# Splitting and moving the one-time ternary rounding of the feed-forward weights in an attention and feed-forward kernel

## What is computed

```python
def absmean_quant(w):
    scale = jnp.mean(jnp.abs(w))
    mask = (jnp.abs(w) >= scale * 0.7).astype(w.dtype)
    return jnp.sign(w) * mask
w1_q = absmean_quant(w1)          # (2048, 512)
w2_q = absmean_quant(w2)          # (512, 2048)
h = gelu(x @ w1_q.T + b1); out = h @ w2_q.T + b2
lambda_full = exp(sum(lq1 * lk1)) - exp(sum(lq2 * lk2)) + LAMBDA_INIT
attn = rmsnorm(attn) * subln_weight * (1.0 - LAMBDA_INIT)   # then @ Wo.T
```

## Time and profile before

| | |
|---|---|
| device time, median of 3 runs | 4300.87 us (4296.52 to 4306.44) |
| device time of the profiled execution | 4298.3 us |
| its span | 4296.5 us |
| busy in it: PE, DVE, ACT, POOL | 3484.7, 3382.8, 2880.2, 1437.2 us |
| mean granted clock of TensorE | 0.926 of full speed |
| block 0 begins at | 87.6 us |

### The profile page before, as it was taken

The page is one execution under the profiler, slowest core; times in us unless marked ns, Lnnn a source line. Parts: engine busy times, 40 slices in busy tenths (PEclk is TensorE's granted clock), DMA queues, the critical chain, the costliest instruction groups (busy, mean ns, idle before and its releaser), DMA issues.

```text
span 4296.5 us, 81536 instructions
## 1 busy us (share of the span) xinstructions
PE 3484.7 (81%) x23454; PEld 2095.0 (49%) x23454; DVE 3382.8 (79%) x6194; ACT 2880.2 (67%) x6784; POOL 1437.2 (33%) x1564
## 2 busy tenths in 40 slices
PE   2688888888888887888788888888878878888886
PEld 1355544455445454545544544445544555444553
DVE  6788977888678886888767887778877889778881
ACT  1577766777567775677756777667766777567772
POOL 1243233332332324433343323432234432333323
PEclk6899999999999999999999999999999999999998
DMA  3100011000011001100011000101011000111000
GB/s 130 41 18 30 19 33 33 31 17 29 25 33 33 18 30 33 33 20 28 21 33 33 26 27 18 39 25 33 20 34 33 25 23 20 34 33 33 15 29 12
DMA packets 146817, 128.38 MB, mean 30 GB/s; under 512 B 66608, under 2 KB 117680, under 8 KB 145840
## 3 DMA queue, kind: packets, MB, share of 16 engines
q1 hardware_dynamic: 146352, 122.79, 8.8%
HBM read 67.61 MB, written 55.12 MB: 29 GB/s over the span
## 4 chain that ended last, share of the span: by engine, by line
PE 41%; DVE 20%; issue 20%; ACT 12%; POOL 5%; DMA 1%; SPq 1%; DVEq 1%; ACTq 1%; POOLq 0%
PE M L837 9%; DVE NM L682 6%; PE M L887 6%; PE SP_ L852 6%; PE F L924 6%; PE F L909 5%; PE DP L864 4%; DVE NM L690 3%; ACT E L554 3%; ACT DT L566 2%; ACT L571 2%; PE M L831 2%; DVE CC L702 1%; PE DX L864 1%; PE SP_ L853 1%
## 5 line engine op out<-in xcount | busy, mean ns | idle before, releaser
L554 ACT ACTIVATE E<-SP_,NM 128x256 f32<-128x256 f32 (+7 forms) x2048 | 1520.4, 743 | 1020.3 <-DVE NM L690 533.8
L852 PE MATMUL SP_<-KST,QST 96*128 96x512 f16 (+3 forms) x3072 | 838.2, 344 | 459.2 <-ACT E L554 385.4
L682 DVE TENSOR_REDUCE NM<-SP_ 128x1 f32<-128x896 f32 (+3 forms) x1024 | 1031.9, 1017 | 225.0 <-PE SP_ L853 218.5
L705 DVE SCALAR_TENSOR_TENSOR E<-E,CC 128x512 f32<-128x512 f32 (+7 forms) x1024 | 942.2, 920 | 36.2
L864 PE MATMUL DP<-ident,E 128*128 128x128 f32 x3328 | 585.1, 292 | 112.8 <-DVE E L705 97.2
L852 PEld LDWEIGHTS SP_<-KST,QST 96*128 96x128 f16 x3072 | 277.9, 101 | 793.8 <-ACT E L554 531.1
L690 DVE TENSOR_REDUCE NM<-SP_ 128x2 f32<-128x1024 f32 (+3 forms) x512 | 419.4, 819 | 244.8 <-PE SP_ L853 239.5
L566 ACT ACTIVATE DT<-DP 128x512 f32<-128x512 f32 (+3 forms) x1024 | 524.8, 513 | 127.8 <-PE DP L864 121.4
L837 PE MATMUL M<-WQKV,WT 128*128 128x512 f32 x1040 | 538.4, 611 | 10.3 <-DVE TOK L746 5.3
L909 PE MATMUL F<-X2H,W1Q 128*128 128x256 f16 x2048 | 501.4, 283 | 39.4 <-ACT HP L613 21.7
L864 PEld LDWEIGHTS DP<-ident,E 128*128 128x128 f32 x3328 | 389.8, 149 | 277.8 <-issue 125.8
(11 more groups left out here) (94 smaller groups left out, 4726.9 us busy)
## 6 DMA issues: line engine op xcount, KB each, us to landing
scratch<-SPL SPq DMA_DIRECT2D x65, 576.0 KB, 2.8
QST<-scratch SPq DMA_DIRECT2D x390, 64.0 KB, 2.4
X<-in_x SPq DMA_DIRECT2D x66, 256.0 KB, 2.7
out<-SQ SPq DMA_DIRECT2D x64, 256.0 KB, 2.0
KST<-scratch SPq DMA_DIRECT2D x390, 32.0 KB, 1.9
DT<-in_w2T SPq DMA_DIRECT2D x1, 4096.0 KB, 25.7
KST<-in_w1T SPq DMA_DIRECT2D x2, 1024.0 KB, 12.0
WQKV<-in_wqT SPq DMA_DIRECT2D x1, 1024.0 KB, 7.1
```

The costliest lines, as they stand in the source:

```text
L554: act.activation(dst, score_out(i, 2 * n + k, w), ACT.Exp, bias=NM[:, (2 * u + k) % 8:(2 * u + k) % 8 + 1], scale=1.0, accum_out=SUM[:, i ...
L682: nc.vector.tensor_reduce(NM[:, m:m + 1], score_out(i, 2 * n + k, P * (i + 1)), AX.X, ALU.max, negate=True).then_inc(max_ready, 1)
L705: nc.vector.scalar_tensor_tensor(out=E1[:, u % 4, 0:w], in0=E2[:, u % 2, 0:w], scalar=CC[:, u % 4:u % 4 + 1], in1=E1[:, u % 4, 0:w], op0=A ...
L852: pe.matmul(SP_[:, k[a // 512], 0:n], q, KST[0:ROWS, a // P:(a + n) // P, kk, :], start=True, stop=not last)
```

## The change

The raw weights go to buffers that are needed later: w1 to DT (tiles 0 to 3), to the upper half of KST (tiles 4 to 7) and to X1, w2 to DT (tiles 4 to 7), HH and HL. The sums of magnitudes are taken by ScalarE (Abs with accumulation). In the setup only chunks 0 and 1 of w1 are cut, by DVE as before. The other two chunks of w1 and all four of w2 are cut inside blocks 0 and 1: the first compare on GpSimd (low_cut), the second on DVE (late_cut). The scaling of Wo, w2's magnitudes and threshold move into block 0. DVE does layernorm before it scales Wq and waits for each load apart; the loads are issued in another order; the clearing of QST moves behind the first rstd on POOL.

```diff
+ABS_AT = (14, 16, 18, 20)
+LOW_AT = ((0, 2), (0, 8), (1, 2), (1, 8), (1, 15), (1, 21))
+CUT_AT = ((0, 6), (0, 12), (1, 6), (1, 12), (1, 20), (1, 26))
+WO_AT, ABS_TOTAL, ABS_PRODUCT, THR_AT = 15, 24, 26, 28
...
+        self.raw = kind == "first"
...
+        kraw = KST[:, TILES // 2:TILES, :, :].rearrange("p a b c -> p (a b c)").bitcast(F32)
+        draw = DT[:, :, :, :].rearrange("p a b c -> p (a b c)")
+        w1f = [draw[:, 0:FF], draw[:, FF:2 * FF], kraw, X1[:, :, :].rearrange("p a b -> p (a b)")]
+        w2f = [draw[:, 2 * FF:3 * FF], draw[:, 3 * FF:4 * FF], HH[:, :, :].rearrange("p a b -> p (a b)").bitcast(F32),
                HL[:, :, :].rearrange("p a b -> p (a b)").bitcast(F32)]
-        cutt = HP[:, :, :].rearrange("p a b -> p (a b)")
+        raw = (w1f, w2f)
+        cut = [q[:, :, :].rearrange("p a b -> p (a b)") for q in (W1Q, W2Q)]
+        low = HP[:, :, :].rearrange("p a b -> p (a b)").bitcast(BF16).rearrange("p (a b) -> p a b", a=2)
...
@ sync: order of the loads is now x, Wq, rope, Wk, Wv, 4 lambda vectors, 4 chunks of w1, Wo, 4 subln_weight, 4 chunks of w2, b1, b2
+                if T.raw and t == TILES // 2 - 1:
+                    sp.wait_ge(cut_done, 4)
...
-            sp.wait_ge(w1_cut, 1)
             sp.wait_ge(q_zeros, 1)
             stack(0, 0, 0, None)
@ gpsimd
+                    if T.raw and (T.t, hs) in LOW_AT:
+                        low_cut(*divmod(LOW_AT.index((T.t, hs)) + 2, 4))
...
+            def low_cut(j, k):
+                n = 4 * j + k - 2
+                pool.wait_ge(raw_in[j][k], 16)
+                pool.wait_ge(thr_ready, j + 1)
+                if n >= 2:
+                    pool.wait_ge(cut_done, n + 1)
+                hold(pool, thr_ready, j + 1)
+                pool.tensor_scalar(low[:, n % 2, :], raw[j][k], thr[:, j, 1:2], 0.0, ALU.is_le, ALU.add).then_inc(low_ready, 1)
+
             rstd(0, 0)
+            pool.memset(QST[:, :, :, :], 0.0).then_inc(q_zeros, 1)
@ scalar
+                    if T.raw and t == 0 and hs in ABS_AT:
+                        abs_chunk(1, ABS_AT.index(hs))
...
+            def abs_chunk(j, k):
+                act.wait_ge(raw_in[j][k], 16)
+                if j:
+                    act.wait_ge(cut_done, 4)
+                hold(act, abs_part, 4 * j + k)
+                act.activation(HP[:, :, :].rearrange("p a b -> p (a b)"), raw[j][k], ACT.Abs,
+                               accum_out=wsum[:, j, k:k + 1]).then_inc(abs_part, 1)
+
             xt_copy(0, 0)
+            for k in range(4):
+                abs_chunk(0, k)
             high(0, 0)
@ vector
+            def cut_chunk(j, k, lows):
+                nc.vector.scalar_tensor_tensor(out=cut[j][:, FF * k:FF * (k + 1)], in0=raw[j][k], scalar=thr[:, j, 0:1],
+                                               in1=lows, op0=ALU.is_ge, op1=ALU.subtract,
+                                               saturate=False).then_inc(cut_done, 1)
+            def late_cut(j, k):
+                n = 4 * j + k - 2
+                dve.wait_ge(low_ready, n + 1)
+                cut_chunk(j, k, low[:, n % 2, :])
...
+                    if T.raw and (t, hs) in CUT_AT:
+                        late_cut(*divmod(CUT_AT.index((t, hs)) + 2, 4))
+                    if T.raw and t == 0 and hs == WO_AT:
+                        dve.wait_ge(wo_in, 16 * 7)
+                        link(nc.vector.tensor_scalar(subc[:, :], subc[:, :], 1.0 - LAMBDA_INIT, None, ALU.mult))
+                        nc.vector.tensor_scalar(WO[:, :, :], WO[:, :, :], subc[:, 0:1], None, ALU.mult).then_inc(wo_ready, 1)
...
-            (the loop over w1 and w2, L792 to L811)
+            abs_total(0)
+            thresholds(0)
+            dve.wait_ge(thr_ready, 1)
+            for k in range(2):
+                link(nc.vector.tensor_scalar(low[:, k, :], raw[0][k], thr[:, 0, 1:2], None, ALU.is_le))
+                cut_chunk(0, k, low[:, k, :])
@ tensor
+                    if T.raw and t == 0 and hs == ABS_PRODUCT:
+                        abs_product(1)
+                    if T.raw and t == 1 and hs == O_PROJ[0]:
+                        pe.wait_ge(wo_ready, 1)
+                    if T.raw and t == 3 and hs == W1_AT[0]:
+                        pe.wait_ge(cut_done, 8)
...
-            pe.wait_ge(ready, 3)
+            abs_product(0)
             every_block(pe, pe_work)
```

More of the change, by code:

```diff
@@ L254, in diff_attention_ffn @@
         scratch = nc.dram_tensor("scratch", [2, P, 3, D + DKV], F16, kind="Internal").ap()
[L257 to L260, removed]
+        wq_in = sem("wq_in")
+        kv_in = sem("kv_in")
+        rope_in = sem("rope_in")
+        lam_in = sem("lam_in")
+        wo_in = sem("wo_in")
+        raw_in = [[sem(f"w{j + 1}_in_{k}") for k in range(4)] for j in range(2)]
+        abs_part = sem("abs_part")
+        thr_ready = sem("thr_ready")
+        low_ready = sem("low_ready")
+        cut_done = sem("cut_done")
+        wo_ready = sem("wo_ready")
         pool_const = sem("pool_const")
@@ L366, in _ @@
                 sp.dma_start(X[:, j, :], x[0, j * P:(j + 1) * P, :]).then_inc(x_in[j], 16)
[L367 to L372, removed]
@@ new lines, in _ @@
+            sp.dma_start(WO[:, :, :], woT.rearrange("k p n -> p k n")).then_inc(wo_in, 16)
+            for j in range(4):
+                sp.dma_start(subc[DV * j:DV * (j + 1), :], subw.unsqueeze(1)).then_inc(wo_in, 16)
+            for k in range(4):
+                sp.dma_start(w2f[k].rearrange("p (k n) -> p k n", k=FT // 4),
+                             w2T[D * k:D * (k + 1), :].rearrange("(k p) n -> p k n", p=P)).then_inc(raw_in[1][k], 16)
+            sp.dma_start(b1c[:, :], b1).then_inc(wo_in, 16)
@@ L706, in diff, with abs_total, thresholds @@
                                                in1=E1[:, u % 4, 0:w], op0=ALU.mult, op1=ALU.add).then_inc(d_ready, 1)
+            def abs_total(j):
+                dve.wait_ge(abs_part, 4 * j + 4)
+                nc.vector.tensor_reduce(wtot[:, j:j + 1], wsum[:, j, :], AX.X, ALU.add).then_inc(abs_sum, 1)
+            def thresholds(j):
+                dve.wait_ge(abs_all, j + 1)
+                link(nc.vector.tensor_scalar(thr[:, j, 0:1], F[:, j:j + 1], 1.0 / (D * FF), TERNARY_CUT, ALU.mult, ALU.mult))
+                nc.vector.tensor_scalar(thr[:, j, 1:2], thr[:, j, 0:1], -1.0, None, ALU.mult).then_inc(thr_ready, 1)
+            def cut_chunk(j, k, lows):
[6 more added lines that the diff above has]
+                cut_chunk(j, k, low[:, n % 2, :])
             def dve_work(T):
@@ L785, in _ @@
             normalise(0, X[:, 0, :], 0, xn_ready)
+            dve.wait_ge(wq_in, 16)
+            nc.vector.tensor_scalar(WQKV[:, :, 0:D], WQKV[:, :, 0:D], DH ** -0.5, None, ALU.mult).then_inc(wq_scaled, 1)
+            dve.wait_ge(lam_in, 16 * 4)
+            link(nc.vector.tensor_tensor(lamp[:, :, :], lamt[:, 0:4:2, :], lamt[:, 1:4:2, :], ALU.mult))
+            nc.vector.tensor_reduce(lams2[:, :], lamp[:, :, :], AX.X, ALU.add).then_inc(lam_prod, 1)
+            dve.wait_ge(rope_in, 16)
             rope_mul(0, 0, 0)
@@ L789, in _ @@
             rest(0, 1)
[L792 to L803, removed]
-                    link(nc.vector.tensor_scalar(cutt, w[k], thr[:, j, 1:2], None, ALU.is_le))
-                    ins = nc.vector.scalar_tensor_tensor(out=qf[:, c], in0=w[k], scalar=thr[:, j, 0:1], in1=cutt,
-                                                         op0=ALU.is_ge, op1=ALU.subtract, saturate=False)
[L807 to L811, removed]
@@ L927, in second_product, with abs_product @@
                     ins.then_inc(f2_ready, 1)
+            def abs_product(j):
+                pe.wait_ge(abs_sum, j + 1)
+                pe.matmul(F[:, j:j + 1], ones[:, :], wtot[:, j:j + 1], start=True, stop=True).then_inc(abs_all, 1)
             def pe_work(T):
@@ L1009, in _ @@
             transposes(T1[:, D:D + DKV], 2, m_kt)
-            for j in range(2):
-                after(pe, abs_sum, j + 1)
-                pe.matmul((F, M)[j][:, 0:1], onesf, wtot[:, j:j + 1], start=True, stop=True).then_inc(abs_all, 1)
-            pe.wait_ge(ready, 3)
+            abs_product(0)
             every_block(pe, pe_work)
```

41 lines of the change are left out of this document (16 added, 25 removed).

## The result

| | before | changed |
|---|---|---|
| median of 12 runs each | 4303.95 us | 4315.12 us |
| lowest and highest | 4296.52, 4307.83 | 4309.89, 4323.95 |
| profiled execution, its span | 4298.3, 4296.5 | 4322.5, 4320.7 |
| mean granted clock of TensorE | 0.926 | 0.920 |

The ratio is 1.0031, 95% interval 1.0021 to 1.0041. 4272.8 was forecast, 4261 to 4285. The two profiled executions lie at the low and at the high end of their kernels' runs, so of the 24.2 us between their spans about half is what the medians show.

A forecast was written before the change was run, and what follows sets the result against it. DVE was taken to bound the stretch from 34 to 87.6 us. The terms -41.7 + 5.5 + 6.2 + 1.9 = -28.1 us, against the median of 4300.87, gave 4272.8 us, range 4261 to 4285.

The forecast's parts named there:

- The new start: Setup: block 0 begins at 45.9 us instead of 87.6, -41.7, with bounds -47.4 to -39.3.
- the write's landing: Setup: the first tile's write to memory, behind loads still moving, lands at 38.0 us; 33.9 if it passed them.
- The four Abs: Setup: ScalarE's sums of w1's chunks stand ahead of high, which starts at 27.1 instead of 22.7, a wait of 4.4 us.
- rival 1: Setup: loads don't hold up the handover's write; block 0 begins at 40.2 to 42, total about 4268; chance 0.08, or better.
- GpSimd's six compares: Blocks 0 and 1: each compare takes 1.94 us on GpSimd without a wait; lengthened VectorE instructions cost +1.9, bounds 0 and 11.6.
- +0.18 for each meeting: Blocks 0 and 1: a two-input VectorE instruction beside a GpSimd tensor_scalar takes 0.53 us instead of 0.35.
- The bound of 11.6: Blocks 0 and 1: upper bound if VectorE stands for the whole of each GpSimd compare, 6 x 1.94 us.
- Rival 4: GpSimd's compare is a slow path, up to 370 us each; VectorE stands at low_ready, kernel near 6500; chance 0.02.
- Blocks 0 and 1: Moved cuts, Abs and Wo's scaling cost +5.5 us in block 0 (+2 to 14.6), cuts +6.2 in block 1 (+4.1 to +9.4).
- All behind block 2 I cost at nothing: Code behind block 2 is untouched by the change and its waits come due long after, so no cost.
- Rival 3: Setup and block 0: Abs needs another table than Exp, loads of 1.283 us, total 4283; chance 0.09 with part of rival 2.
- about -40 and -16: Whole kernel: gains in us with two terms at a time at their bounds, from which the range was drawn.

The follow-up runs named there:

- e7_handover: e2_dve_low with QST cleared before the first rstd, high and rest before the last two Abs, unneeded loads after the handover; 4278.27 us, 0.9931 of the kernel before.
- e3_low_mult: Changed kernel with GpSimd's is_le compare replaced by a multiply with the same operands, so six chunks are not rounded as the reference does; 4292.16 us, ratio 0.9978.
- e2_dve_low: Changed kernel with all six late first compares done by VectorE instead of GpSimd; 4287.66 us, ratio 0.9966 to the kernel before.
- e5: Changed kernel with 15 more semaphore increments at the head of VectorE's program; 4316.00 us, ratio 1.0012 to the kernel before.
- e8: Kernel before with 241 more semaphore increments at the head of VectorE's program; 4326.38 us, ratio 1.0038.
- e1: Kernel before with two unused tensors, so later tensors lie at the changed kernel's addresses; 4304.62 us, ratio 1.0005.
- e6: Kernel before with 18 more semaphore increments at the head of GpSimd's program; 4312.56 us, ratio 1.0003.
- e4: Kernel before with two more multiplies of Wo by 1 at the end of its setup; 4305.61 us, ratio 1.0009.

## Why the prediction was wrong, point by point

The forecast was -28.1 us and the medians give +11.2, 39.3 us more. By the points below some 25 of them are GpSimd's compares, some 10 what lies behind block 2, and 3 the new start.

**The new start (-41.7): right in kind, -38.6 measured.** The end of the chain, the read of KST, and VectorE's being done earlier (39.1 forecast, 40.2 measured) were right. Three terms were small by some us: the first projection at 14.49 and not 10.2, since the clearing of QST, which I called free because POOL's next task came late, stopped VectorE instead; ScalarE's high at 28.67 and not 27.1; the write's landing at 41.8 and not 38.0. The four Abs, priced as a wait of 4.4 us, cost high only 1.2: the late projection had made the transposed q itself late (27.46 and not 22.7). e7_handover mends them together and wins 9.3 us, 6.2 of them at the landing; rival 1, a write that passes the loads, is refuted by the 9.0 us.

**GpSimd's six compares (+1.9): the step that failed.** "I take 1.94, since a compare and a multiply are the same instruction with another operation" is wrong: six rows of 7.15 to 9.07 us, 45.1 in sum for 11.6; e3_low_mult pins it on the operation (1.98 us with a multiply, so the 1.94 was a fair price for that one). All GpSimd tensor_scalars in the trace of before are multiplies with an add of 0, so no row there could price a compare. And "+0.18 for each meeting" was wrong in its form. These VectorE instructions don't slow down a little beside GpSimd, they stand for most or all of its instruction: 4.58, 4.47, 4.72 us for a difference beside is_le, 1.97 beside a multiply, and 7.12 for a one-input normalise beside a mere clearing. The earlier trace rows had it: the instruction of 0.35 that took 1.08 started during this one of GpSimd and ended 0.16 us behind it, a price that grows with the neighbour's length. Timeline of GpSimd in the kernel before:

```profile
101.97 1.26 POOL L455 TENSOR_TENSOR T<-T 128x512 f32<-128x512 f32 x1 [11.09 <-DVE T L665]
```

The bound of 11.6 was counted right for standing, but with the wrong length; with the measured one it would have been 45. Blocks 0 and 1 lost 39.4 us in the changed kernel (38.6 won, 0.8 behind at the third load) for a forecast of 13.6. Less the 12.4 us of the cuts and Abs (next but one point) that leaves 27.0 for the six compares, near the 28.0 by which the rows are longer, where the forecast had 1.9.

The Trainium skill, "SBUF — State Buffer" (Terms), says that the pair of ports that VectorE and GpSimd share is an exclusive lock, held for the full instruction, and that the loser fully blocks. The normalises agree (7.12 us beside the clearing, 2.80 us up to the end of a compare), and so does the difference beside the multiply (1.97 us). The differences beside is_le agree only in part: they are done 2.3 to 2.5 us before the compare's row ends, and a cut runs at full pace in what is left of one. Why is not shown; how exact the ends of GpSimd's rows are isn't either. I had weighed the milder wording of another page.

**Rival 4 was the right one, with the wrong price and the wrong point of decision.** It was given 2 in 100, up to 370 us a compare, and "decides from some 9 us a compare on", because I had VectorE wait only at low_ready. 7.2 us sufficed, since VectorE stands in differences and normalises as well. At the third load of x the changed kernel is level with before (0.8 us behind); what makes it slower in the end comes behind that.

**Blocks 0 and 1 (+5.5 and +6.2): about right.** e2_dve_low has no GpSimd compare: 37.5 won at the start (50.15 for 87.6), 17.4 left at the third load, so 20.1 paid, of which 7.7 are VectorE's own compares: 12.4 for a forecast of 11.7. In sum, cuts, Abs and Wo's scaling cost what was said; their parts were not measured apart, and some of it may be the clock, which is granted at 0.75 from the second to the third load of x in e2_dve_low and at 0.86 before.

**"All behind block 2 I cost at nothing": wrong, by some 10 us.** The instructions there are the same, but 15 fewer VectorE instructions stand ahead of the loop. That this place matters for the second block is shown: 15 idle instructions take the late row maximum, the longer pause and the clock's drop away (e5), 241 bring the long second block back (e8), and addresses, GpSimd's code and a begin 2.6 us later do not bring it (e1, e6, e4). That it is the whole loss in the loop is likely, not shown: the three kernels with 901 instructions, and only they, lose 0.18 to 0.25% there, but each with an uncertainty of about 0.1%, and e8, with 9.1 us in its second blocks, shows none. Why the place matters is argued only: a stop of VectorE's instruction fetch would fit. The Trainium skill ("Runtime: NRT & Kernel Launch", Instruction fetch mechanics) says that code is fetched in blocks of 256 instructions, and that the cost of crossing into the next is mostly hidden; e8, 256 further, shows the second block's sign again, but not the loss in its total, so the period stays open. Open as well is what in e7_handover's loop is better than before.

**Rival 3** (table loads) is out: ScalarE shows no load at the Abs, whose price (1.91 and 0.19 us) was right.

**The range** was drawn too narrow by its own terms: it goes by two terms at a time, "about -40 and -16". With the two worst, block 0 and GpSimd, at their bounds the sum is -28.1 + 9.1 + 9.7 = -9.3, which is 4292; with the two best it is -37.3. The measured time lies outside that as well.

## What to carry to other kernels

Work moved to GpSimd was here not beside VectorE but in front of it: VectorE's differences (two inputs) and normalises stood for most or all of a GpSimd instruction that had begun before them, so a long one can cost most of its length on a VectorE path, whatever GpSimd's own slack. Reductions and 128x1 instructions ran on. Price an operation on an engine by that operation, not by one of the same form; where no row has it, try one instruction of it first, or leave the work where its price is known. Before the last microseconds of a loop are explained by what was changed in it, look whether code ahead of it has only shifted it: here 15 idle instructions at an engine's head were enough to tell.

## What the runs showed of the hardware

- GpSimd's tensor_scalar over 128x2048: multiply and add, or add and multiply, 1.97 to 1.98 us; is_le and add 7.15 to 7.17; max and min (bf16 input) 7.07 to 7.12, where nothing held them up.
- A clearing of 128x8192 f16 on GpSimd, 6.92 us, stopped a VectorE tensor_scalar of 512 columns for 7.12 us. Beside a compare of 7.41 us VectorE's row maximum (one input, from PSUM) and a reduction of 512 columns kept their length: 0.69 us at 124.19 and 0.68 at 124.80.
- Beside GpSimd's is_le VectorE's two-input differences were done 2.3 to 2.5 us before the end of the compare's row, one-input normalises at its end.
- A write of 576 KB issued behind loads of 4 MB on the same queue landed in 9.0 us, and in 2.8 with those loads behind it.
- The place of VectorE's loop code moved one row maximum by 0.35 us; TensorE's pause behind it grew to 1.52 us, the granted clock fell, and the block took up to 2.4 us more.
